# Causal sixteen-head attention: the four value packs of a group issued as two runs of two packs

## What is computed

```
Q, K, V = x @ Wq + bq, x @ Wk + bk, x @ Wv + bv     # h = norm(x) stands for x
Q, K = rope(Q, K)                                   # layer 1: no rope, no biases
scores = einsum('bhqd,bhkd->bhqk', Q, K)
scores = where(causal, -inf, scores)
attn = softmax(scores / sqrt(8), axis=-1)
ctx = einsum('bhqk,bhkd->bhqd', attn, V)            # 16 heads, 512 x 512 per head
return ctx @ Wo + bo
```

## Time and profile before

| | us |
|---|---|
| median of 3 runs | 6337.89 (6331.5 to 6341.06) |
| the profiled execution, its time | 6336.72 |
| its span in the profile | 6334.9 |
| first causal stage (layer 0), first position to last pack | 153 to 758 |
| second causal stage (layer 1) | about 1258 to 1908 |

### The profile page before, as it was taken

The page is one execution under the profiler, slowest core; times in us unless marked ns, Lnnn a source line. Parts: engine busy times, 40 slices in busy tenths (PEclk is TensorE's granted clock), DMA queues, the critical chain, the costliest instruction groups (busy, mean ns, idle before and its releaser), DMA issues. The chain is left out here.

```text
span 6334.9 us, 118561 instructions
## 1 busy us (share of the span) xinstructions
PE 5123.1 (81%) x38207; PEld 2643.1 (42%) x38217; DVE 3519.6 (56%) x5633; ACT 3125.7 (49%) x7068; POOL 2547.7 (40%) x2162
## 2 busy tenths in 40 slices
PE   5999779788885999998799998884226999975995
PEld 2444334233332656563465664353101322232784
DVE  5777432376664656554566664466337988821233
ACT  1666633256563655552365664343012877841542
POOL 3333010222213878761687883105563322116125
PEclk7999989889996999999899999996556999977997
DMA  3344211143320000001000000002102333211123
GB/s 96 101 105 106 57 40 50 43 105 97 94 70 21 6 7 7 8 2 82 19 7 6 6 4 5 2 1 65 34 7 75 90 94 83 74 46 46 54 75 90
DMA packets 317744, 313.51 MB, mean 49 GB/s; under 512 B 85382, under 2 KB 242722, under 8 KB 315298
## 3 DMA queue, kind: packets, MB, share of 16 engines
q1 hardware_dynamic: 300834, 285.80, 16.7%
q0 software_dynamic: 16384, 20.69, 1.2%
HBM read 172.15 MB, written 136.32 MB: 49 GB/s over the span
## 5 line engine op out<-in xcount | busy, mean ns | idle before, releaser
L714 ACT ACTIVATE a_prob<-a_PB 128x512 f32<-128x512 f32 x2304 | 1252.1, 596 | 527.5 <-PE a_PB L590 396.8
L638 PE MATMUL a_PO<-a_prob,a_V 128*32 128x256 f32 (+3 forms) x8192 | 726.9, 428 | 20.1 <-ACT a_cn L687 19.9
L822 DVE TENSOR_REDUCE a_blocks<-a_PA 128x8 f32<-128x1024 f32 x512 | 608.4, 1215 | 137.9 <-PE a_PA L590 137.6
L825 DVE TENSOR_REDUCE a_neg<-a_PA 128x2 f32<-128x1024 f32 x512 | 591.5, 1212 | 52.2 <-PE a_PA L603 52.2
L603 PE MATMUL a_PA<-a_KS,a_QS 48*128 48x512 bf16 (+3 forms) x3072 | 477.1, 350 | 158.5 <-DVE a_blocks L822 44.3
L2409 DVE TENSOR_REDUCE f1a_neg<-f1a_PA 128x2 f32<-128x384 f32 (+1 forms) x512 | 266.6, 521 | 479.2 <-PE f1a_PA L2211 467.0
L2339 POOL TENSOR_TENSOR f1a_prob<-f1a_prob,f1a_inv 128x384 f32<-128x384 f32 (+1 forms) x512 | 394.5, 773 | 318.5 <-DVE f1a_inv L2413 318.4
L620 PE MATMUL a_PB<-a_QS,a_KS 51*128 51x512 bf16 (+3 forms) x3072 | 453.4, 332 | 71.4 <-ACT a_prob L714 42.3
L2303 ACT ACTIVATE f1a_pt<-f1a_PT 128x512 f32<-128x512 f32 (+1 forms) x512 | 278.4, 544 | 361.8 <-PE f1a_PT L2220 358.5
L2296 ACT ACTIVATE f1a_prob<-f1a_PA,f1a_neg 128x192 f32<-128x192 f32 (+1 forms) x1024 | 405.5, 404 | 95.2 <-DVE f1a_neg L2409 95.2
L603 PEld LDWEIGHTS a_PA<-a_KS,a_QS 48*128 48x128 bf16 x3072 | 119.9, 95 | 699.2 <-issue 333.5
(11 more groups left out here) (442 smaller groups left out, 10338.4 us busy)
## 6 DMA issues: line engine op xcount, KB each, us to landing
a_spill<-a_qkp SPq DMA_DIRECT2D x576, 128.0 KB, 2.4
a_QS<-a_spill SPq DMA_DIRECT2D x384, 96.0 KB, 2.6
a_KS<-a_spill SPq DMA_DIRECT2D x384, 96.0 KB, 2.7
a_raw<-a_cn SPq DMA_DIRECT2D x192, 72.0 KB
f_rows<-tokens_in SPq DMA_DIRECT2D x78, 128.0 KB
tokens_out<-f_rows SPq DMA_DIRECT2D x78, 128.0 KB
tokens_in<-f1g_zero SPq DMA_DIRECT2D x9, 1024.0 KB, 13.9
a_heads<-a_raw SPq DMA_DIRECT2D x32, 256.0 KB, 3.3
```

The lines of the kernel that those rows point to most:

```text
L638: mm = nc.tensor.matmul(PO[32 * j:32 * j + 32, first:last], V[:, par, t, 8 * e + pr], prob[:, k % st.ring, e, c + first - q0:c + last - q0 ...
L714: nc.scalar.activation(prob[:, k % st.ring, e], PB[:, ring_b.slot(0, ("b", s, e))], ACT.Exp, scale=scale).then_inc(pb_used, 1)
L822: nc.vector.tensor_reduce(to, of, AX, ALU.max).then_inc(pa_used, 1)
L825: nc.vector.tensor_reduce(neg[:, t, pr], PA[:, bank:bank + 2], AX, ALU.max, negate=True).then_inc(pa_used, 1)
```

## The change

In the causal table, pack 0 moves from position at+4 to at+5, and pack 3 from at+6 to at+7. Packs 0 and 1 then stand together, and so do 3 and 2. The order 0, 1, 3, 2, what each pack waits for, the evacuation and all other engines' programs stay as they are.

```
-                self.packs += [(g, 0, at + 1, at + 4, 2), (g, 1, at + 3, at + 5, 2), (g, 3, at + 3, at + 6, 2), (g, 2, at + 4, at + 7, 2)]
+                self.packs += [(g, 0, at + 1, at + 5, 2), (g, 1, at + 3, at + 5, 2), (g, 3, at + 3, at + 7, 2), (g, 2, at + 4, at + 7, 2)]
```

## The result

| | before | after |
|---|---|---|
| median of six runs of each, taken together | 6339.48 us | 6382.71 us |
| the profiled execution's span | 6334.9 us | 6380.3 us |
| first causal stage, first position to last evacuation | 649.2 us | 677.7 us |
| second causal stage, the same | 650.4 us | 665.7 us |

A stage's time runs from the start of its first a position (109.1 us in before; the 153 us given for the first stage above is its first b position) to the start of its last evacuation. The ratio is 1.0073, with a 95% interval of 1.0057 to 1.0090. The change makes the kernel slower by 43 us in the medians and by 45.4 us between the two profiled executions.

What follows compares the result with a forecast made beforehand. The bound changes by slot: TensorE's work, ScalarE's exponentials (1.15 to 1.26 us) or transfers. First stage 14, second stage 14 and clock -3 made +25 us, 6362 us; range 6338 to 6382.

Steps and rivals of the forecast that it cites:

- E→M: Piece of a step from the evacuation of group 3 to the product M: forecast 1.07 us longer.
- two in three: Clock behind M's 1.88 us idle: share of falls assumed in the first stage's eight waiting steps, 6 us together.
- 0→E: Position 0 to the evacuation of group 3: forecast 0.41 us longer in the first stage, 0.85 in the second.
- the 0.72 that I gave to slower: Whole kernel: chance of slower by over 0.2%, joining the forecast (0.60) and the slower rival (0.12).
- Packs 0 and 1 together about 1.85 us: Sign to look for in the new trace: the joined run of packs 0 and 1 takes about 1.85 us.
- The terms for the ends: Four batches at each stage's ends, no wait holding delay: 2 us each, 8, in the first; 1.5 each, 6, second.
- first stage, waiting steps, clock in it: Eight steps whose position 0 waits for transfers: 8 x (0.41 + 0.2) = 4.9 us, plus 6 for clock falls.
- first stage, loop-head steps: Four steps with a 3 to 4 us gap at the loop's head, where M doesn't wait: 0.4 each, 1.5 us.
- second stage, waiting and loop-head steps, clock in it: Eight waiting steps 6.8 us, four loop steps 1.2, clock +1, and -10 for old falls gone.
- slot arithmetic: Pricing slots without transfer waits: ScalarE holds emptied ones at 1.25 us; pack 0 leaving saves 0.64, arriving adds 0.85.
- M→0: Piece of a step from the product M to position 0: forecast sum of slot changes -0.02 us.
- slower by more: Rival: idle at M drops the clock in nearly all 22 steps, old drops stay; +40 us, 6377; chance 0.12.

Runs made afterwards that it cites:

- p3only: Against the kernel before, only pack 3 moved, from at+6 to at+7 beside pack 2: ratio 0.9987.
- g2: Against the kernel before, the change made in group 2 alone (its packs 0 and 3 moved): ratio 1.0030.
- filler: The changed kernel plus four products of 512 columns into M's own bank ahead of M's wait: ratio 1.0055 against the kernel before.

## Why the prediction was right in sign and short in size

**What held.** The emptied slots are ScalarE's (1.16 and 1.24 us, and 1.02 with half the exponential). A run of two pays for its columns only. E→M grows by 1.07 us. M waits 1.7 to 2.0 us in 22 steps, and the clock falls at 13 of them, near the two in three that I took. The second stage's four falls behind transfers at position 0 are gone, and six behind M came in their place. The waits for the transfers there shrank by more than half (19.3 to 8.6 us), where I had said a third. 0→E grows by 0.89 us in the second stage (5.36 to 6.25; I had 0.85). The outcome fell in the 0.72 that I gave to slower. "Packs 0 and 1 together about 1.85 us" was a slip: that is the sum of the two alone, and with the join's saving my own numbers give 1.64. The terms for the ends, 2 us each in the first stage and 1.5 in the second, are the wrong way round by my own pieces (1.07 - 0.02 + 0.41 and + 0.85); their sum stays at 14.

**What was short.** The stages' growth, 43.8 us, by the terms of the sum (differences of single profiled executions, so each is good to a microsecond or two):

| term | forecast | measured |
|---|---|---|
| first stage, waiting steps, clock in it | 4.9 + 6 | 13.5 |
| first stage, loop-head steps | 1.5 | 2.6 |
| first stage, ends | 8 | 12.4 |
| second stage, waiting and loop-head steps, clock in it | 6.8 + 1.2 + 1 - 10 | 0.7 |
| second stage, ends | 6 | 14.6 |
| outside the two stages | 0 | 1.6 |

Two terms were mis-sized, and the second is the step that failed.

(1) **Position 0 to E in the first stage: 0.41 forecast, 0.76 measured.** I took 0.44 us off for pack 3, which leaves a slot with a Q product behind it, by the sentence "there pack 3 takes 0.35 + 0.09 away". The rows of before:

```profile
465.00 1.13 PE L661 MATMUL a_PA<-H,a_wqk 128*128 x2
...
467.20 1.13 PE L661 MATMUL a_PA<-H,a_wqk 128*128 x2
```

In before the two Q products are 2.20 us apart with pack 3 between them; in after they are 2.08 apart without it (477.45 and 479.53 above), and the second has waited 0.16 us for VectorE's copy of the first out of the banks that a positions use too. A third pacer stood right behind the one that I removed: 0.12 us came back and not 0.44. p3only, where only pack 3 leaves that slot, says the same: 0→E went from 6.32 to 6.22 us. Over 12 steps that is 12 x 0.35 = 4 us, as much as the first two rows of the table lack (3.7).

(2) **The ends: 14 forecast, 27.0 measured.** This is the larger part. The sum gave the batches at a stage's ends the slot arithmetic (2 and 1.5 us each) and put the clock there at nothing: it counted falls only in the eight waiting steps. But the ends have a bare M too, no wait for a transfer takes up what a fall costs there, and a fall is dearer than 1.5 us. After, end of the first stage:

```profile
742.63 0.59 PE L651 MATMUL a_PB<-ident_b,a_mp 128*48 128x128 bf16 x4 [1.83 <-DVE a_mp L843]
...
743.86 3.21 PE L638 MATMUL a_PO<-a_prob,a_V 128*32 128x512 f32 x16
```

```profile
742.58:751.00 8.42, 8.37 (x66) 2.95 (x66) 0.75 (x1) 3.83 (x8) 0.00 (x0) 0.63 0.03 8
```

The clock is 0.63 over 8.4 us. M→0 took 10.73 us here and 7.63 in the same step of before, +3.1. The ends of each stage are four pieces: from its start to the first evacuation of group 3, the last two steps, and what lies behind them. Four of the eight have a fall at M (at 182.6, 742.6, 1868.9 and 1909.7), with M→0 longer by 3.2, 3.1, 3.4 and 2.0 us; these pieces grew by 4.6, 4.95, 4.7 and 5.4 us, the four without a fall by 1.0, 1.8, 2.1 and 2.3, near the 1.5 to 2 us of the slot arithmetic. With some 3 us for each fall the ends would have been 14 + 12 = 26.

The step of the forecast that failed is thus the price of the ends, 8 + 6 us, which measured 12.4 + 14.6. Its premise, "the other four batches, at the ends, have no wait that holds anything", was right, and for that very reason the clock had to be added there in full. The rival "slower by more" (+40, chance 0.12) came out nearest in time, but not by its reason: the falls did not come in nearly all steps, and the old ones of the second stage did not stay on top (granted clock of the whole stage 0.91 before and 0.92 after).

The Trainium skill, page TensorEngine Tiling (Array Packing), section Tiling Modes, has the switch of mode drain TensorE. The trace agrees in kind (39.7 us less busy time in L638), and the slower kernel shows that a saving on TensorE need not be one of time. The Trainium skill's page Perfetto Trace Analysis, section Matmul Optimizations, asks for products back to back in batches because the engine's power follows its use. The change made larger batches and, at M, larger holes: M waits 1.7 to 2.0 us in place of 0.5 to 1.0, and the clock fell in 13 of 22 such steps, where before it fell in none.

## What to carry to other kernels

When work is moved to join it with its like, price the slot that it leaves by its second pacer, and the third, before counting the saving: here TensorE waited 61 us more for ScalarE, and VectorE took back 0.3 us a step in another slot. Joining by moving work earlier, into waits and ahead of the path's last stretch, gained 0.2 to 0.4%, where joining by moving it later lost 0.7%. And price a stage's first and last steps by themselves, with every penalty that the steady state hides.

## What was not expected of the hardware

- The clock behind waits of the same length: 1.00 behind 1.89 us at 455.76 in g2, 0.50 behind 1.81 us at 219.93. It fell at none of the 202 waits at M that were 1.23 us or shorter, a stage's first M left out.
- A fall cost 1.5 us in the run of packs alone (3.15 us against 1.65), and about 3 us at a stage's end (M→0 10.73 against 7.63).
- Idle time removed in one place brought falls in another (filler, first stage, loop: none at an M with added products, two behind position 0). By the granted clock from the stage's second M on, the low stretches of the first stage make some 31 us in before, 47 in after and 34 in filler; in the second stage 72, 68 and 58. So the change moved the falls of the second stage more than it added to them.
